# Attention weights turned by one transposing DMA per pair of heads instead of two, with a third buffer of 16-bit parts

## What is computed

```python
q = (inputs @ w_q.T).reshape(b, t, H, HD)        # H = 16 heads of HD = 16
k = (inputs @ w_k.T).reshape(b, t, H, HD)
v = (inputs @ w_v.T).reshape(b, t, H, HD)
scores = jnp.einsum('bqhd,bkhd->bhqk', q, k)
scores = jnp.where(causal, -jnp.inf, scores)
attn = jax.nn.softmax(scores / scale, axis=-1)
ctx = jnp.einsum('bhqk,bkhd->bqhd', attn, v).reshape(b, t, D)
return ctx @ w_o.T + b_o
...
x = x + 0.5 * _L0_ffn_ref(_layernorm(x, axis=-1), ...)
x = x + _L0_attn_ref(_layernorm(x, axis=-1), ...)
x = x + 0.5 * _L0_ffn_ref(_layernorm(x, axis=-1), ...)
```

## Time and profile before

| | us |
|---|---|
| median of 3 runs | 424.38 |
| the 3 runs | 421.07 to 424.41 |
| the profiled execution | 425.93 |
| its span | 424.2 |

### The profile page before, as it was taken

The page is one execution under the profiler, slowest core; times in us unless marked ns, Lnnn a source line. Parts: engine busy times, 40 slices in busy tenths (PEclk is TensorE's granted clock), DMA queues, the critical chain, the costliest instruction groups (busy, mean ns, idle before and its releaser), DMA issues.

```text
span 424.2 us, 9276 instructions
## 1 busy us (share of the span) xinstructions
PE 386.5 (91%) x2732; PEld 313.3 (74%) x2733; DVE 297.4 (70%) x620; ACT 256.7 (61%) x640; POOL 236.0 (56%) x307
## 2 busy tenths in 40 slices
PE   8879999999999989597898997887899999999996
PEld 4548888888888857366666766564688888888885
DVE  6877999555666797876777586968356775556666
ACT  2736875566555555888897797722355555655553
POOL 5155445565567359557877487200555555654860
PEclk9889999999999999989998898999999999999999
DMA  8949922112111710377757667727741211111126
GB/s 280 371 115 391 378 79 63 52 37 74 49 49 37 257 55 0 75 113 138 121 117 131 96 125 117 130 42 255 224 144 51 63 53 49 62 49 51 48 92 229
DMA packets 71953, 51.57 MB, mean 122 GB/s; under 512 B 54128, under 2 KB 65648, under 8 KB 71664
## 3 DMA queue, kind: packets, MB, share of 16 engines
q1 hardware_dynamic: 67088, 37.00, 33.8%
q0 software_dynamic: 4544, 12.07, 9.3%
q10 hardware_dynamic: 288, 2.10, 1.3%
HBM read 29.37 MB, written 9.19 MB: 91 GB/s over the span
## 4 chain that ended last, share of the span: by engine, by line
PE 66%; DVE 18%; DMA 7%; issue 4%; ACT 3%; POOL 1%; DVEq 0%; SPq 0%; ACTq 0%; POOLq 0%
PE bank L1398 28%; PE bank L1420 14%; PE bank L1570 4%; PE bank L1408 4%; DMA pT<-parts 4%; DVE parts L1204 3%; PE bank L1319 3%; DVE neg_max L1190 3%; PE bank L1374 2%; PE bank L1537 2%; DMA arena<-xn_scratch,gather_row 2%; PE bank L1609 1%; DVE v L1274 1%; PE bank L1340 1%; ACT bank L806 1%
## 5 line engine op out<-in xcount | busy, mean ns | idle before, releaser
L540 POOL DMA_INDIRECT arena<-xn_scratch,gather_row x46 | 49.3, 1071 | 69.4 <-PE bank L1374 47.9
L546 POOL DMA_INDIRECT y_scratch<-arena,scatter_row x42 | 63.0, 1499 | 38.9 <-ACT arena L709 37.7
L1398 PE MATMUL bank<-w_hi,xT_hi 128*128 x184 | 62.4, 421 | 0.0
L1048 DVE TENSOR_TENSOR wo_lo<-w_out,wo_hi 128x1024 fp32r<-128x1024 f32 x46 | 56.4, 1225 | 4.4 <-PE bank L1420 2.3
L1053 DVE TENSOR_TENSOR gT_lo<-bank,gT_hi 128x512 fp32r<-128x512 f32 x46 | 31.7, 690 | 37.7 <-ACT gT_hi L683 37.7
L1398 PE MATMUL bank<-w_hi,xT_lo 128*128 x184 | 58.0, 396 | 0.0
L1398 PE MATMUL bank<-w_lo,xT_hi 128*128 x184 | 57.7, 395 | 0.0
L676 ACT ACTIVATE arena<-bank 128x512 f32<-128x512 f32 x46 | 27.5, 597 | 46.2 <-PE bank L1398 44.9
L621 POOL TENSOR_TENSOR k_head<-k_hi,head_mask 128x256 fp32r<-128x256 f32 x64 | 38.7, 625 | 27.7 <-PE bank L1571 26.0
L1570 PE MATMUL bank<-k_head,xT_hi 128*128 128x256 f32 (+1 forms) x128 | 41.4, 406 | 12.9 <-DVE parts L1204 11.8
L698 ACT ACTIVATE wo_hi<-w_out 128x1024 fp32r x46 | 48.8, 1061 | 5.7 <-issue 3.2
(11 more groups left out here) (193 smaller groups left out, 916.1 us busy)
## 6 DMA issues: line engine op xcount, KB each, us to landing
w_raw<-in_win_t SPq DMA_DIRECT2D x8, 1024.0 KB, 9.4
w_out<-in_wout_t SPq DMA_DIRECT2D x16, 512.0 KB, 10.4
w_out<-y_scratch SPq DMA_DIRECT2D x8, 512.0 KB, 5.0
xn_scratch<-arena ACTq DMA_DIRECT2D x2, 1024.0 KB, 7.1
x<-in_x SPq DMA_DIRECT2D x4, 256.0 KB, 3.4
pT<-parts SPq DMA_TRANSPOSE x64, 3.3
out<-x SPq DMA_DIRECT2D x4, 256.0 KB, 2.2
arena<-xn_scratch,gather_row POOLq DMA_INDIRECT x46
```

Of the source, the lines that this page charges most:

```text
L540: pool.indirect_dma_start(out=xb[j % 2][:, :], out_offset=None, in_=xn_dram, in_offset=bass.IndirectOffsetOnAxis(ap=gather_row[:, j:j + 1] ...
L546: pool.indirect_dma_start(out=y_dram, in_=y[j % 2][:, :], in_offset=None, out_offset=bass.IndirectOffsetOnAxis(ap=scatter_row[:, j:j + 1], ...
L1048: dve.tensor_tensor(wo_lo[:, :, :], w_out[:, bass.ds(e, 1), :, :].rearrange("p o c d -> p (o c) d"), wo_hi[u][:, :, :].bitcast(F32), ALU.s ...
L1398: last = pe.matmul(bank[2 * half + u][:, :], tok[u][:, k, :], wts[:, bass.ds(e, 1), k, half * H:(half + 1) * H], start=(part == 0 and k == ...
```

## The change

The two transposing DMAs of a pair become one of twelve tiles, with one semaphore per parity (`pT_ready`) in place of two. It is issued when the low parts of both tail and head are there. The parts buffers now hold high and low apart (`[P, 2, 6, P]`), so the tile numbers in `high`, `low` and `weigh` change, and nothing in their sizes. There is a third parts buffer, `parts_late`. It lies where `v_rest` lay, which is in use while the values are split, so pair 4 is the first to use it and waits for `v_ready` to do so; from pair 5 on, `high` waits for the DMA of pair g - 3 instead of g - 2. The order of the instructions on PE, ACT, DVE and POOL is the same as before, the weighing behind both scores of its step included; `pT` still has two buffers.

```diff
-            v_rest = [room_sb(f"v_rest{u}", [P, HEADS, HD]) for u in range(VSLOTS)]
+            with ExitStack() as inner_room:
+                v_rest = [inner_room.enter_context(nc.sbuf_tensor(f"v_rest{u}", [P, HEADS, HD], F32)) for u in range(VSLOTS)]
+            parts_late = room_sb("parts_late", [P, 2, 3 * 2, P], F16)
...
-            parts = [room_sb(f"parts{u}", [P, 2 * 3 * 2, P], F16) for u in range(2)]
+            parts = [room_sb(f"parts{u}", [P, 2, 3 * 2, P], F16) for u in range(2)]
+            parts.append(parts_late)
...
+        def parts_of(g):
+            return parts[g if g < 2 else (g - 2) % 3]
...
             def turn_parts(g):
                 u = g % 2
-                for n, (tiles, turned) in enumerate(((slice(0, 8), tail_turned[u]), (slice(8, 12), head_turned[u]))):
-                    sp.wait_ge(low_ready, g * 2 + n + 1)
-                    if g > 1 and n == 0:
-                        sp.wait_ge(pv_done, g * 2 - 2)
-                    sp.dma_start(pT[u][:, tiles, :], parts[u][:, tiles, :].rearrange("p t k -> p (t k)"), transpose=True)\
-                        .then_inc(turned, 16)
+                sp.wait_ge(low_ready, g * 2 + 2)
+                if g > 1:
+                    sp.wait_ge(pv_done, g * 2 - 2)
+                sp.dma_start(pT[u][:, :, :], parts_of(g)[:, :, :, :].rearrange("p a t k -> p (a t k)"), transpose=True)\
+                    .then_inc(pT_ready[u], 16)
...
             def high(b, s):
-                used = b * (16 * HPAIRS // 2) + (s - SLAG - 1) // 2 * 16
-                reach(act, tail_turned[u], used)
+                if g == 4:
+                    act.wait_ge(v_ready, TILES)
+                elif g > 1:
+                    user = g - 2 if g < 4 else g - 3
+                    act.wait_ge(pT_ready[user % 2], user // 2 * 16 + 16)
                 act.wait_ge(tail_probs_ready, g * 2 + 2)
...
-                reach(act, head_turned[u], used)
                 act.wait_ge(head_probs_ready, g * 2 + 2)
...
             def weigh(b, s):
-                pe.wait_ge(tail_turned[(s - 1) % 2], used)
-                pe.wait_ge(head_turned[(s - 1) % 2], used)
+                pe.wait_ge(pT_ready[g % 2], g // 2 * 16 + 16)
```

More of the change, by code:

```diff
@@ L110, in build @@
             v = room_sb("v", [P, TILES, HEADS, 3 * HD], BF16)
-            v_rest = [room_sb(f"v_rest{u}", [P, HEADS, HD]) for u in range(VSLOTS)]
+            with ExitStack() as inner_room:
+                v_rest = [inner_room.enter_context(nc.sbuf_tensor(f"v_rest{u}", [P, HEADS, HD], F32)) for u in range(VSLOTS)]
+            parts_late = room_sb("parts_late", [P, 2, 3 * 2, P], F16)
+            room_sb("rest_place", [P, HEADS, HD])
             with ExitStack() as inner_room:
@@ L333, in build @@
         low_ready = sem("low_ready")
-        tail_turned = [sem(f"tail_turned{u}") for u in range(2)]
-        head_turned = [sem(f"head_turned{u}") for u in range(2)]
+        pT_ready = [sem(f"pT_ready{u}") for u in range(2)]
         pv_done = sem("pv_done")
@@ L819, in high @@
                 u = (s - 1) % 2
-                used = b * (16 * HPAIRS // 2) + (s - SLAG - 1) // 2 * 16
-                reach(act, tail_turned[u], used)
+                if g == 4:
[3 more added lines that the diff above has]
+                    act.wait_ge(pT_ready[user % 2], user // 2 * 16 + 16)
                 act.wait_ge(tail_probs_ready, g * 2 + 2)
-                act.activation(parts[u][:, 0:4, :], bank[u][:, :].rearrange("p (t k) -> p t k", t=4), ACT.Copy,
+                act.activation(parts_of(g)[:, 0, 0:4, :], bank[u][:, :].rearrange("p (t k) -> p t k", t=4), ACT.Copy,
                                scale=P_SCALE).then_inc(high_ready, 1)
-                reach(act, head_turned[u], used)
                 act.wait_ge(head_probs_ready, g * 2 + 2)
-                act.activation(parts[u][:, 8:10, :], bank[2 + u][:, 0:2 * P].rearrange("p (t k) -> p t k", t=2), ACT.Copy,
+                act.activation(parts_of(g)[:, 0, 4:6, :], bank[2 + u][:, 0:2 * P].rearrange("p (t k) -> p t k", t=2), ACT.Copy,
                                scale=P_SCALE).then_inc(high_ready, 1)
@@ L1200, in low @@
                 u = (s - 1) % 2
-                high, rest = (slice(0, 4), slice(4, 8)) if tail else (slice(8, 10), slice(10, 12))
+                tiles = slice(0, 4) if tail else slice(4, 6)
                 source = bank[u][:, :] if tail else bank[2 + u][:, 0:2 * P]
                 dve.wait_ge(high_ready, g * 2 + (1 if tail else 2))
-                dve.scalar_tensor_tensor(parts[u][:, rest, :], source.rearrange("p (t k) -> p t k", k=P), P_SCALE,
-                                         parts[u][:, high, :], ALU.mult, ALU.subtract).then_inc(low_ready, 1)
+                dve.scalar_tensor_tensor(parts_of(g)[:, 1, tiles, :], source.rearrange("p (t k) -> p t k", k=P), P_SCALE,
+                                         parts_of(g)[:, 0, tiles, :], ALU.mult, ALU.subtract).then_inc(low_ready, 1)
             def add_up(b):
@@ L1584, in weigh @@
                     both, second = slice(2 * HD * h, 2 * HD * (h + 1)), slice(2 * HD * h + HD, 2 * HD * (h + 1))
-                    for i, rest, (qt, kt) in ((8 + hh, 2, (0, 0)), (2 * hh, 4, (1, 0)), (2 * hh + 1, 4, (1, 1))):
+                    for i, (qt, kt) in ((4 + hh, (0, 0)), (2 * hh, (1, 0)), (2 * hh + 1, (1, 1))):
                         rows = v[:, bass.ds(b * 2 + (kt - 2 * ago), 1), h, :]
@@ L1589, in weigh @@
                         pe.matmul(to[:, second], turned[:, i, :], rows[:, :, 2 * HD:3 * HD], start=False, stop=False)
-                        last = pe.matmul(to[:, both], turned[:, rest + i, :], rows[:, :, 0:2 * HD], start=False, stop=(kt == qt))
+                        last = pe.matmul(to[:, both], turned[:, 6 + i, :], rows[:, :, 0:2 * HD], start=False, stop=(kt == qt))
                     last.then_inc(pv_done, 1)
```

1 line of the change is left out of this document (removed).

## The result

| | before | changed |
|---|---|---|
| median of 20 runs | 424.06 us | 420.82 us |
| lowest to highest | 419.98 to 429.07 | 419.08 to 422.92 |
| the profiled execution | 425.93 | 420.87 |
| its mean granted clock | 0.975 | 0.990 |

The ratio is 0.9945, 95% interval 0.9922 to 0.9969: 0.55% faster, or 2.3 us (the medians differ by 3.2). That is less than the 1% named ahead, but it is a gain, and the forecast was a loss of 1.6 us. Ratios and means here leave out the runs that lie over 1.5% above the fastest of the same kernel (two of the twenty above, ten of the 105 runs of the kernel before that stood beside the experiments, and two of other kernels), which is one reason why the medians differ by more.

The account below looks back on a forecast made before the run. The attention loop was taken as bound by handing over between engines. Terms -0.5, +0.4, +0.2 and +0.5 gave +0.6 us, disturbed transfers +1.0: +1.6 on the median, 426.0 us, range 420.5 to 431.5.

Parts of the forecast that it names:

- the three pieces: Attention loop stretches from low part of pairs 5, 13, 21 to scores of 12, 20, 28; each 14.41 us.
- ACT's 5.0 us go: ACT's waits on the transposing DMA before writing high parts, 5.0 us in four places, fall to about nothing.
- The transfer, issue 1.25 and landing 4.0: The twelve-tile transposing DMA occupies SP's queue for 1.25 us and lands after 4.0 us.
- critical pairs: Pairs 5, 8, 13, 16, 21, 24, 31, the seven places where a late transfer was said to cost time.
- The line through two sizes: Landing of four tiles (2.6 us) and eight (3.3) extended to twelve: 0.7 us more, so 4.0.
- The pieces become 14.41: Each path of two transfers, weighings and scores, behind pairs 5, 13 and 21, takes 14.41 us after the change.
- the first piece: Low part of pair 5 to scores of 12: from 14.90 to 14.41 us, a gain of 0.5.
- the second was to lose 0.4: Low part of pair 13 to scores of 20: from 14.02 to 14.41 us, a loss of 0.4.
- The third was to lose 0.2: Low part of pair 21 to scores of 28: from 14.19 to 14.41 us, a loss of 0.2.
- The middle and the end: Between the pieces of the loop nothing changes; the last pair's landing comes later, costing 0.5 us in full.
- One of the late transfers hits a critical pair, +1.0: Of four late transfers that ACT felt before, one falls among seven binding pairs of the loop, costing 1.0 us.
- The clock as a rival for slower only: PE's new waits before pairs 5, 13, 21 bring more TensorE clock falls, 2.1 us each: 431 us, chance 0.15.

Follow-up runs that it names:

- the second pair: One further profiled execution each of the unchanged kernel before and the changed kernel, nothing else altered; spans 422.7 and 418.4 us.

## Why the prediction was wrong

It gave 426.0 with a range of 420.5 to 431.5, and no change within 1% as the likeliest. The time lies in the range and within that 1%, though just inside its lower end, and it moved the other way, 0.55% under before instead of 0.4% over. The step that failed is the sum of the three pieces: its path was right, but each piece was put at 14.41 us, and the undisturbed ones measured 13.8; three smaller terms leaned the same way. In the order of its steps:

- *ACT's 5.0 us go.* Right: no such wait is left, and the third buffer alone makes the whole gain.
- *The transfer, issue 1.25 and landing 4.0.* Mis-sized a little. The issue takes 1.43 as the median, landing 3.6 to 3.9, and 3.88 and 3.87 at the critical pairs 13 and 16. The line through two sizes was too steep: from eight to twelve tiles it is 0.3 to 0.6 us, not 0.7. By the rate in the Trainium skill ("DMA: Bandwidth & Descriptors", section "Anatomy of one DMA — SWDGE (gpsimd) path"), put on top of the 3.3 us of eight tiles, it was to be 3.6, an estimate; with the page's fixed part as well, 2.0 + 0.9 for 393 KB, it would be 2.9, an estimate too, which no landing reached. The lowest landings are 3.6, and the critical ones lie nearer to the line's 4.0, so neither held.
- *The pieces become 14.41.* This is the step that failed. The path was right, with all its links, and the sum too high by 0.63: 4.56 us from the low part of 13 to the scores of 17 (forecast 4.85), 4.58 on to the low part of 16 (4.71), 4.64 to the scores of 20 (4.85). The transfers make 0.25 of it, the step between 0.13, and the rest are the links: from low part to issue 0.03 us where 0.05 was taken, from landing to the first weighing 0.04 at pair 13 where 0.14 was, and nothing beside the weighing's 0.6 where another 0.05 was added. The gain of the first piece was to be 0.5 and is 1.1 to 1.4; the second was to lose 0.4 and gains 0.2. The third was to lose 0.2 and lost 0.4 in the execution without a fall in it (against 13.88).
- *The middle and the end.* Right that nothing changes between scores of 12 and 20 and the low part behind them (11.62 to the hundredth). From the scores of 28 to the low part of 31 the change was put at nothing and is a gain of half a microsecond (15.15 against 15.69 in the second pair): in that execution of the kernel before a late transfer held ACT for 1.2 us there. The end was to cost 0.5 and costs 0.1: the last transfer had landed 3.73 us behind its low part, where 4.05 were forecast and 3.54 stood before.
- *One of the late transfers hits a critical pair, +1.0.* Half right. In the changed kernel the landings of over 4.4 us (from the low part) fell on pairs 7, 10, 15, 21, 23 and 28: one critical pair, late by 0.5, and that is what it cost in the execution without a fall (14.24 where the piece behind 13 took 13.76). Pairs 10 and 23, with 5.4 and 5.9, cost nothing that ACT or the chain shows.
- *The clock as a rival for slower only.* It moved the other way. The prediction counted only new falls by PE's waits, and gave no chance to fewer than before. Mean clock over the runs went from 0.983 to 0.991, and PE's ten waits of 10.3 us brought no more falls than there were. Its price was wrong as well: 2.1 us was that of a double stretch (6.83 us). Within the runs of either kernel, 0.01 more of granted clock goes with 2.2 and 2.0 us less, from which one stretch of 3.41 us is worth 0.8 to 0.9 us, an estimate.

With the pieces as measured the sum is -1.1 - 0.2 + 0.4 - 0.5 + 0.05 = -1.4 us (rounded) in place of +1.6, without any change in the clock. The rest of the 2 us between the means, and how much of the whole the clock carries, isn't settled: filling PE changes the two kernels unequally, and some of the falls that differ lie where the kernels are the same. That the time fell within the range all the same is luck: the range was drawn for other causes.

## What to carry to other kernels

Ask of a buffer which transfers are late now and who stands behind them; a third buffer takes up what a single late one costs. Take the links between two engines from rows too: hundredths and tenths of a microsecond in each, three pieces over, turned the sign of a change as small as this one. When transfers are joined or split, compare the issues of a burst of steps with the length of the burst on the issuing queue, not only the landing of one. Before a fall of TensorE's clock is put down to a wait, look whether a second execution has it too, and whether falls differ where the kernels don't. And one measurement of a pair of kernels can be off by half a per cent here; two builds that share the suspected part are the better witness.

## What was unexpected of the hardware

- A transposing DMA of eight tiles takes 3.3 us to landing, twelve 3.6 to 3.9, and each of two with six tiles 2.8: the size counts little, the number of issues on one queue (1.2 to 1.5 us each) counts.
- The transfers that are late are nearly the same in both executions of one kernel, and others in another kernel: pairs 15 and 23 take 4.6 and 5.9 us from low part to landing in both profiled executions of the changed kernel, pair 6 takes 5.4 in both of the kernel before, where pair 23 takes 3.8, and pair 6 takes 3.75 in the changed one. The instruction queue has 17 packets in both kernels. In the changed one each of its seven packets between 170 and 270 us falls within a transfer that took over 4 us from its issue, two of them (at 205.9 and 246.9) within the latest, of 5.4 and 5.1. But no run here took them away, and other transfers were late without one, so that cause stays a candidate.
- TensorE's clock falls in stretches of 3.41 us (or two in a row) in all these traces, to 1.2 GHz; where one begins differs between executions of one kernel (in the attention at 181.36, 229.15 and 259.87 in the first of before, at 181.6 and 202.08 in the second; in the changed kernel at 172.13 and 243.81, and at 178.74 alone). One in the attention's first steps, at 171 to 182 us, is in all fifteen profiled executions.
